# Self attention of a two-layer decoder step in the context attention's form: queries and keys split through DRAM, scores twice, the maximum added by a product

## What is computed

```python
# L1_xattn: 16 heads over the 361 context rows, then L1_ffn, which begins with self attention:
q = (src @ Wq).reshape(Bb, Tt, H, DH).transpose(0, 2, 1, 3)
k = (src @ Wk_c @ Wk).reshape(Bb, Tt, H, DH).transpose(0, 2, 1, 3)
v = (src @ Wv_c @ Wv).reshape(Bb, Tt, H, DH).transpose(0, 2, 1, 3)
q = _apply_rope(q, sin, cos)
k = _apply_rope(k, sin, cos)
attn = jnp.einsum('bhqd,bhkd->bhqk', q, k) / np.sqrt(DH).astype(np.float32)
attn = jax.nn.softmax(attn, axis=-1)
sa = jnp.einsum('bhqk,bhkd->bhqd', attn, v)
sa = sa.transpose(0, 2, 1, 3).reshape(Bb, Tt, C) @ Wo
x = _rmsnorm(src + sa, norm1_w)
# then a shared FFN, 8 experts in 2 groups, and a last rmsnorm
```

## Time and profile before

| | us |
|---|---|
| runs of the kernel before | 538.31, 544.36, 545.44; median 544.36 |
| span of the profiled execution, first to last instruction | 534.7 |
| busy in it: PE, DVE, ACT, POOL | 500.6, 276.7, 187.7, 161.2 |
| context attention's last two quads, 315.8 to 323.0 | 7.2 |
| self attention, 323.0 to 397.1 | 74.1 |

### The profile page before, as it was taken

How to read it: one execution, slowest core, us unless ns; L and a number is a source line. 1 busy time by engine, 2 the same in 40 slices (tenths; PEclk the granted TensorE clock), 3 DMA queues, 4 the chain that set the end, 5 groups by cost and what they waited for, 6 DMA issues and landing times.

```text
span 534.7 us, 9480 instructions
## 1 busy us (share of the span) xinstructions
PE 500.6 (94%) x3452; PEld 335.8 (63%) x3452; DVE 276.7 (52%) x664; ACT 187.7 (35%) x444; POOL 161.2 (30%) x180
## 2 busy tenths in 40 slices
PE   9989898999998969999999988899999899999991
PEld 8556654454566657788877767787866575444441
DVE  3466651221227475656676877988654226223352
ACT  2343231211114345555555564556662104200000
POOL 3130123011126044332231562543201467100242
PEclk9999999999999998999999999999999999999997
DMA  5999994499877697885664209400000153111100
GB/s 138 265 277 313 385 348 127 158 361 392 310 244 219 147 252 170 209 234 139 173 163 97 54 1 331 143 2 3 1 1 1 42 150 113 41 37 54 27 12 24
DMA packets 52588, 82.33 MB, mean 154 GB/s; under 512 B 10910, under 2 KB 41126, under 8 KB 52541
## 3 DMA queue, kind: packets, MB, share of 16 engines
q1 hardware_dynamic: 45788, 69.05, 43.5%
q0 software_dynamic: 5776, 12.13, 7.2%
q10 hardware_dynamic: 976, 0.53, 0.4%
HBM read 66.87 MB, written 15.15 MB: 153 GB/s over the span
## 4 chain that ended last, share of the span: by engine, by line
PE 78%; DVE 11%; issue 4%; DMA 2%; POOL 2%; ACT 2%; POOLq 0%; SPq 0%; DVEq 0%; ACTq 0%
PE pb L1551 72%; DVE hN L1111 1%; DVE nmx L1412 1%; POOL xs_dram L656 1%; DVE prob L1415 1%; PE pb L1990 1%; DMA hN<-yt_dram 1%; PE pb L1849 1%; PE pb L1759 1%; DVE ctxbuf L1342 1%; DVE nmx L1320 1%; PE pb L1561 1%; DVE x L1263 1%; PE pb L1723 1%; DMA xs_dram<-arena,slot 1%
## 5 line engine op out<-in xcount | busy, mean ns | idle before, releaser
L1551 PE MATMUL pb<-split 128*100 128x362 f32 (+2 forms) x320 | 77.3, 325 | 6.4 <-DVE nmx L1320 2.7
L1551 PE MATMUL pb<-ring,big 128*116 (+1 forms) x232 | 76.8, 578 | 0.0
L1320 DVE TENSOR_REDUCE nmx<-pb 100x1 f32<-100x361 f32 x128 | 62.7, 527 | 24.2 <-PE pb L1551 23.8
L1551 PEld LDWEIGHTS pb<-split 128*100 128x100 f32 (+2 forms) x320 | 54.7, 179 | 16.4 <-issue 5.7
L1551 PEld LDWEIGHTS pb<-ring,big 128*116 128x116 f32 (+1 forms) x232 | 31.2, 162 | 42.0 <-issue 40.9
L987 ACT ACTIVATE big<-pb 121x400 f32<-121x400 f32 (+1 forms) x96 | 48.1, 504 | 22.5 <-PE pb L1551 19.9
L721 POOL TENSOR_TENSOR shift<-consts,nmx 100x400 fp32r<-100x400 f32 x32 | 28.2, 882 | 77.6 <-DVE nmx L1320 77.5
L1551 PE MATMUL pb<-big,arena 121*32 121x100 f32 (+3 forms) x1072 | 47.9, 264 | 1.7 <-ACT arena L835 1.2
L1551 PEld LDWEIGHTS pb<-big,arena 121*32 121x32 f32 (+3 forms) x1072 | 29.1, 113 | 18.4 <-issue 6.9
L1551 PE MATMUL pb<-shift 100*121 100x400 f32 (+1 forms) x96 | 34.6, 361 | 0.0
L1551 PE MATMUL pb<-hT,wgu 128*128 128x400 f32 (+1 forms) x100 | 33.0, 469 | 1.3 <-DVE big L1205 1.0
(11 more groups left out here) (277 smaller groups left out, 839.7 us busy)
## 6 DMA issues: line engine op xcount, KB each, us to landing
ring<-in_L_ffn_gate_up_proj SPq DMA_DIRECT2D x12, 1024.0 KB, 9.5
split<-kx_dram SPq DMA_DIRECT2D x64, 181.0 KB, 4.1
ring<-in_L_ffn_down_proj SPq DMA_DIRECT2D x12, 512.0 KB, 7.6
kx_dram<-split POOLq DMA_DIRECT2D x16, 362.0 KB, 5.1
ctxbuf<-in_L_ffn_gate_up_proj SPq DMA_DIRECT2D x4, 1024.0 KB, 8.9
ring<-in_L_ffn_W_experts SPq DMA_DIRECT2D x4, 1024.0 KB, 12.7
ctxbuf<-in_ctxT SPq DMA_DIRECT2D x10, 361.0 KB
split<-qx_dram SPq DMA_DIRECT2D x64, 50.0 KB, 2.1
```

Source lines behind the costliest of these rows:

```text
L1320: nc.vector.tensor_reduce(nmx[:, t % 4, q:q + 1], PB[SB[n % 3]][0:T, 0:CTX], AX.X, ALU.max, negate=True) \
L1551: return nc.tensor.matmul(o, l, r, start=start, stop=stop)
```

## The change

The self attention takes the context attention's form. The features of queries and keys are put by parity of the head, as those of the context, by a permutation of the weights on the host; so the rotation's partner is 8 rows away (`SWAP_PAIRS`). After the addition ACT rounds a part to its high part (`high_parts`), POOL subtracts it for the low part (`low_part`), SP stores both to DRAM by `store_self` in four DMAs, and `load_self(g)` brings a group of two batches back in twelve. PE's `self_scores(n)` are four fp32r products of 100 columns, made two units ahead; `self_shifted(n)` makes the transposed scores with the maximum added, by two products of 200 columns and one of 400; the exponential goes from PSUM straight to `pT4`. DVE only takes the maximum (`self_max`), POOL builds the diagonal matrices (`self_minus_max`). The spread of the queries, DVE's addition, the transposes and their copies go. The tables of pieces and rotations are changed, four memsets clear the query buffer in quads 20 to 23, and the weights of the FFN are loaded later: the shared ones after `load_self(3)`, those of the experts after the last unit.

```diff
-              (28, "middle"): ("V", 1, 0), (28, "end"): ("V", 2, 0), (30, "middle"): ("g", 2, 0), (31, "middle"): ("Q", 1, 0)}
+              (28, "middle"): ("V", 1, 0), (28, "end"): ("V", 2, 0), (30, "middle"): ("g", 2, 0), (30, "end"): ("Q", 1, 0),
+              (31, "middle"): ("Q", 1, 1), (31, "end"): ("C", 1, 0)}
+LATE_SELF = {0: ("n", NB - 1, 0), 1: ("K", 1, 0), 2: ("t", NB - 1, 0), 3: ("y", NB - 1, 0), 4: ("K", 1, 1), 5: ("V", 3, 0),
+             6: ("V", 4, 0), 7: ("g", 3, 0), 8: ("Q", 2, 0), 9: ("Q", 2, 1), 10: ("C", 2, 0), 11: ("K", 2, 0), 12: ("K", 2, 1),
+             13: ("V", 5, 0), 14: ("Y", 0, 0), 15: ("V", 6, 0), 16: ("Y", 1, 0), 18: ("V", 7, 0), 19: ("Y", 2, 0), 23: ("Y", 3, 0),
...
-ROTATE_SWAP = [24, 25, 26, 30, NQUAD + 5, NQUAD + 8, NQUAD + 14, NQUAD + 18]
-ROTATE_ADD = [26, 28, 29, NQUAD + 1, NQUAD + 7, NQUAD + 11, NQUAD + 17, NQUAD + 21]
+ROTATE_SWAP = [24, 25, 26, 28, NQUAD - 1, NQUAD + 5, NQUAD + 10, NQUAD + 13]
+ROTATE_ADD = [26, 28, 29, 30, NQUAD + 2, NQUAD + 7, NQUAD + 12, NQUAD + 15]
+NSTAGE = 3
...
 # SP
+            def store_self(r):
+                w, g = ROTATE[r]
+                sp.wait_ge(s("d_lo"), r + 1)
+                for odd in range(2):
+                    for hl in range(2):
+                        sp.dma_start(self_dram[w][2 * g:2 * g + 2, odd, hl].rearrange("b p t -> p b t"),
+                                     qk_parts[:, r % NSTAGE, hl, odd, :].rearrange("p (b t) -> p b t", t=T).bitcast(f32)) \
+                            .then_inc(s(QK_STORED[r % NSTAGE][0]), 16)
+
+            def load_self(g):
+                for w in "qk":
+                    r = ROTATE.index((w, g))
+                    name, base = QK_STORED[r % NSTAGE]
+                    sp.wait_ge(s(name), base + 64 * (r // NSTAGE + 1))
...
+            store_self(0)
+            store_self(1)
+            store_self(2)
+            sp.wait_ge(s("filled"), FILL["self_queries"])
+            load_self(0)
+            store_self(3)
             sp.wait_ge(s("c_st"), NJ * NQUAD)
+            load_self(1)
+            store_self(4)
+            store_self(5)
+            sp.wait_ge(s("c_st"), SELF_3 + 2 * NG)
+            load_self(2)
+            store_self(6)
+            store_self(7)
+            sp.wait_ge(s("c_st"), SELF_3 + 4 * NG)
+            load_self(3)
...
 # POOL
+            def low_part(r):
+                w, g = ROTATE[r]
+                pool.wait_ge(s("d_hi"), r + 1)
+                t = (qT if w == "q" else krT)[:, :, 2 * T * g:2 * T * (g + 1)]
+                nc.gpsimd.tensor_tensor(qk_parts[:, r % NSTAGE, 1], t, qk_parts[:, r % NSTAGE, 0].bitcast(f32), ALU.subtract) \
+                    .then_inc(s("d_lo"), 1)
+
+            def rotations(t):
+                for r in range(len(ROTATE)):
+                    if t == ROTATE_ADD[r] + 1:
+                        low_part(r)
+                for r in range(len(ROTATE)):
+                    if t == ROTATE_SWAP[r] + 1:
+                        times_cos(r)
...
+            for n in range(4 * NB):
+                self_minus_max(n)
...
+                rotations(NQUAD + n)
...
 # ACT, in unit n
+                act.wait_ge(s("c_st"), SELF_3 + n + 1)
...
+                nc.scalar.activation(pT4[0:T, n % 2, :], PB[ST[n % 2]][0:T, 0:4 * T], ACT.Exp).then_inc(s("c_p"), 1)
+                high_parts(NQUAD + n)
...
 # PE
+            def self_shifted(n):
...
+                for u in range(2):
+                    at = T * (2 * g + u)
+                    mm(PB[ST[n % 2]][0:T, 2 * T * u:2 * T * u + 2 * T], k_slot[:, b % 2, at:at + T],
+                       q_slot[:, b % 2, :, at:at + T], u == 0, False)
+                pe.wait_ge(s("c_diag"), NQUAD + n + 1)
+                mm(PB[ST[n % 2]][0:T, 0:4 * T], ones_r[:, 0:T], diag[:, n % 2, :], False, True).then_inc(s("c_st"), 1)
...
                     scores(4 * (t + AHEAD) + 3)
+                else:
+                    self_scores(t + AHEAD - NQUAD)
                 if t >= 1:
                     weighted_values(t - 1)
...
+            for n in range(4 * NB):
+                for w, c, i in bank6_self(n):
+                    bank6_part(w, c, i)
+                self_shifted(n)
+                if n + AHEAD < 4 * NB:
+                    self_scores(n + AHEAD)
+                if g == 0 and b >= 2:
+                    d_turn_back(b - 2)
+                if n >= 1:
+                    self_weighted(n - 1)
```

264 lines of the change are left out of this document (150 added, 114 removed), and 4 rows, old and new, of the table LATE_SELF.

## The result

| | before | after |
|---|---|---|
| time, us, median of four runs each | 543.53 (538.31 to 545.44) | 574.79 (571.61 to 579.37) |
| span of the profiled execution | 534.7 | 574.3 |
| granted clock, mean | 0.987 | 0.942 |

The ratio is 1.062, with a 95% interval of 1.054 to 1.070 (the quotient of the medians, 1.058, lies in it): slower by 31 us between the medians. The forecast was 556.9 with a range to 568.0; the direction held, the size didn't.

A forecast was written before the change was run, and what follows sets the result against it. It took self attention as bound by TensorE; 11.8 + 1.7 - 7.4 + 5.5 + 0.9 + 1.8 - 1.8 = +12.5 us on a span of 534.7 gave 547.2, and with 9.7 added 556.9 us, range 541 to 568.

The forecast's parts named there:

- What bounds it: Self attention, 323.0 to 397.1 us: bound by TensorE, busy 69.5 of 74.1 us, with 4.6 us of short waits.
- The unit, -7.4: TensorE's work per unit of four heads: 1.22 us in place of 1.45, 32 times, -7.4 us.
- The start, +11.8: PE at scores of unit 0 waits for group 0's store and load, 317.5 to 329.3: +11.8 us (10 to 14).
- The clock after it, +1.7: Behind the first wait, half of a 3.5 us stretch lost to a slow clock: +1.7 us (0 to 3.4).
- The low parts, +5.5: Low parts of rotations 4 to 7 on POOL delay the next product: four waits, +5.5 us (2 to 8).
- The cosine products, +0.9: Three cosine products on POOL at n = 6, 11, 14 stand ahead of a product, wait for nothing: 0.3 each, +0.9 us.
- The roots, 0: Norm roots in the self attention's units: the prediction gave them no term.
- The late load, +1.8: Scores of unit 24, reached in n = 22, wait for load_self(3): +1.8 us (0 to 4); load_self(2) just hidden.
- Pieces, -1.8: Waits at pieces among the units, 2.8 us, against the 4.6 us idle before: -1.8 us.
- A: Rival: the first scores' wait and cold clock, 13.5 us, shrink; 543.4 us with no wait, chance 0.20.
- C: Rival: POOL's product with the maximum paces every unit; 0.3 us a unit more, +10, 567 us, chance 0.13.
- D: Rival: one-pass scores bring nothing, each costs 0.18 us, the unit 1.58; 568.4 us, chance 0.08.

The follow-up runs named there:

- e6: Changed kernel with each group's queries loaded as soon as they are stored, only key loads waiting for the keys' store; 566.88 us, 1.048 times before.
- e1: Changed kernel with self attention loads taking the context's stored queries, without waiting for the stores (output not the reference's); 548.35 us, 1.013 times before.
- e5: e1 with the last four low parts left out, their stores following the high parts (output not the reference's); 540.85 us (532.04 to 545.48).
- e10: Changed kernel with first scores later, queries loaded ahead, group 0 keys and last pieces earlier, last low parts and three cosine products on DVE; 551.75 us, 1.017 times before.
- e11: Changed kernel with only the last three cosine products moved from POOL to DVE; 577.00 us (570.77 to 583.93), quicker runs 1.059 times before.
- e7: Changed kernel with the last four low parts moved from POOL to DVE, behind its maximum of the same unit; 577.14 us, 1.064 times before.
- e3: Changed kernel with the low parts of rotations 4 to 7 one unit later on POOL; 578.75 us, 1.066 times before.
- e12: e5 with the last three cosine products on DVE (output not the reference's); 540.78 us over ten runs, 1.000 times before.

## Why the prediction was wrong, step by step

- **What bounds it: right.** TensorE and its waits make the whole difference.
- **The unit, -7.4: right, a little small.** 1.17 us in place of 1.22: -9.0 (9 to 11 by the table). My 0.09 for a 100-column score was borne out: four of them at 417.81 take 0.40 until the next instruction starts. The 44 ns come from a formula that the Trainium skill (TensorE: Matmul & The Clock Gate, section Back-to-back issue gap) gives for an isolated matmul; for a stream in which each matmul brings new weights the same section has about 81 ns at 128 columns, and says that the formula under-counts there. These rows, 0.10 us each, are nearer to that, and the prediction should have named it.
- **The start, +11.8: 15.0, the mechanism right, the landing mis-sized.** From PE's readiness the last key store's issue began at 1.0 and ended at 3.0 us where I had 2.1, its landing (first load issued at 4.8) fits my 4.4, the issue of the loads took 5.1 as forecast. But I gave the last load 2.1 us to land, from loads of 50 KB each, where these have 100 and 200, and it took 5.4. I had named the heavier key loads as the upper bound (14.1 us of wait); for twelve loads of 1.6 MB in a row the bound was the likelier end, and e6, which takes away a half of the bytes and most of the issue, gave back 4.0 us. The measured wait lies above even that bound.
- **The clock after it, +1.7: 11.4, the step that failed worst, 9.7 us short.** I took one stretch of 3.5 us behind one wait. In the trace half clock followed the first wait, then came back behind the 1.59 us wait at 380.50, in the late wait, and behind the 1.77 at 425.71. The forecast had further waits in its own sum and gave them no clock. Nor is it the long waits that bring it: e1 has none of them and 13.5 us of clock. By e5 against e1 a stretch can get 8.3 us shorter where its waits differ by 0.7. In every trace of the new form the half clock costs 6 us or more, where the sum had 1.7; what decides how much is open (below).
- **The low parts, +5.5: 3.6.** Three waits (0.77, 1.06, 1.74) in place of four; the residual piece covered the one at n = 14.
- **The cosine products, +0.9: 2.7.** I wrote that they wait for nothing. They wait for DVE's shuffle, with the next diagonal matrix behind them:

```profile
378.22 1.42 POOL L753 TENSOR_TENSOR tT<-tT,consts 128x400 f32<-128x400 f32 x1 [2.57 <-DVE ctxbuf L1429]
379.60 1.66 POOL L827 TENSOR_TENSOR shift<-consts,nmx 100x400 fp32r<-100x400 f32 x2
```

  and PE's product stood at 380.50 with 1.59 of waiting. The product took 1.42, not the 1.04 that I used, though the earlier trace rows show that too. e10 and e11, which move these products away, lose the waits of 1.13 and 1.59.
- **The roots, 0: 1.8.** The norm's root at n = 28 stands ahead of product 29 in the same way. I hadn't costed it, since it was there before; before, no product stood behind it. The wait of 1.77 is the same in all the experiments.
- **The late load, +1.8: 7.1.** The last load landed 5.9 us after its issue in place of 2.1, which is 3.8 of the missing 5.3; the rest isn't assigned. That load_self(2) was "just hidden" came out to 0.1 us, and by luck: half clock just ahead of it held PE back by some 3 us (see e7). It is the place where gains ahead of it came back (e3, e7, e9).
- **Pieces, -1.8: -0.3.**
- **The sum.** 32.3 less 12.5 is 19.8 us: the clock 9.7, the late load 5.3, the start 3.2, cosine products and root 1.8 each, the pieces 1.5, less 1.6 for the unit and 1.9 for the low parts.
- **The rivals.** A (short round trip) is refuted, e1 shows what it would have been worth. C's condition, that POOL paces each unit, did not come: units without company ran at 1.17 us, and the product took 0.87 in the mean, about as in the earlier trace rows. The row of 2.59 that the prediction names there does not bear on instructions with two tensor inputs, since this one reads one tensor and two scalars per row (`hN<-x,mv,rstd`); two such rows took 0.73 in the changed kernel at 317.51, with no spread product beside them. D is refuted. None held the clock or the landing under load, and the range ended 7 us too low for that.

Left open: what brings the half clock. It came at 331.4 in e12, behind waits of 0.58 and 1.29 us, and at 330.5 in e1; the same two waits in the changed kernel (to 349.67 and 354.32) had none behind them, nor had the 1.74 us to 395.39. The kernel before has waits of 1.03, 1.16 and 0.91 us in its own stretch and kept full clock there, in the one quick execution that was profiled. So the length of a wait alone doesn't tell. A variant of the kernel before with such waits wasn't tried.
